# Softmax reciprocals that ride in the maximum's transposes and are spread over 128 partitions by a transfer inside SBUF

## The reference

```python
q = _lora_linear(hidden_states, Wq, Aq, Bq)      # 8 x 256 x 1024 -> 32 heads of 32
k = _lora_linear(traces, Wk, Ak, Bk)             # 8 heads, each serves 4 query heads
v = _lora_linear(traces, Wv, Av, Bv)
scores = jnp.einsum('bhqd,bhtd->bhqt', q, k) / jnp.sqrt(jnp.asarray(HD, q.dtype))
attn = jax.nn.softmax(scores, axis=-1)
context = jnp.einsum('bhqt,bhtd->bhqd', attn, v)
out = _lora_linear(context, Wo, Ao, Bo)
return hidden_states + out
```

## Time and profile before

| what | value |
|---|---|
| median of 3 runs | 734.06 us (733.98 to 735.76) |
| the profiled execution | 734.93 us |
| its span | 733.1 us |
| PE busy | 715.6 us (98%) |
| DVE busy | 465.7 us (64%) |
| ACT busy | 446.6 us (61%) |
| POOL busy | 246.4 us (34%) |

### The profile page before, as it was taken

One profiled execution on the slowest core, in us unless ns is written; L12 is line 12 of the kernel. 1 busy time (PEld: TensorE's weight loads), 2 busy tenths in 40 slices (PEclk: granted clock), 3 DMA queues, 4 the chain that ended last, 5 costly groups with the idle time before them and its releaser, 6 DMA issues.

```text
span 733.1 us, 15768 instructions
## 1 busy us (share of the span) xinstructions
PE 715.6 (98%) x5248; PEld 611.6 (83%) x5248; DVE 465.7 (64%) x833; ACT 446.6 (61%) x1418; POOL 246.4 (34%) x246
## 2 busy tenths in 40 slices
PE   6989999999999999999999999999989999999998
PEld 6768888888888888888888888888757788888886
DVE  4947877787777777678678778778876321222211
ACT  3547788788878878878788878788976211011100
POOL 3662731550641245165134406505456300000000
PEclk8999999999999999999999999999989999999999
DMA  6777663465356346435735733654674533454231
GB/s 234 268 226 191 186 178 120 123 195 174 109 179 199 124 152 188 142 98 176 202 109 157 200 122 115 196 175 137 188 228 138 187 129 113 161 172 138 91 114 57
DMA packets 94785, 117.10 MB, mean 160 GB/s; under 512 B 8736, under 2 KB 76320, under 8 KB 94752
## 3 DMA queue, kind: packets, MB, share of 16 engines
q1 hardware_dynamic: 94752, 116.69, 51.0%
HBM read 78.91 MB, written 37.75 MB: 159 GB/s over the span
## 4 chain that ended last, share of the span: by engine, by line
PE 89%; DVE 4%; ACT 3%; DMA 2%; issue 1%; POOL 1%; SPq 0%; DVEq 0%
PE banks L1043 34%; PE banks L1116 23%; PE banks L1061 9%; PE banks L1105 9%; PE banks L1086 8%; PE banks L1096 2%; PE banks L1077 2%; ACT banks L706 1%; PE banks L1028 1%; DMA probs_t<-b4kv 1%; DVE w_sum L827 1%; PE banks L1030 1%; DVE neg_max L857 1%; POOL k_stack L583 1%; DMA probs_t<-wq 1%
## 5 line engine op out<-in xcount | busy, mean ns | idle before, releaser
L706 ACT ACTIVATE banks<-banks,neg_max 128x256 f32<-128x256 f32 x512 | 229.2, 449 | 63.5 <-DVE neg_max L857 63.5
L857 DVE TENSOR_REDUCE neg_max<-banks 128x2 f32<-128x512 f32 x256 | 175.7, 687 | 53.0 <-PE banks L1061 51.0
L717 ACT ACTIVATE probs_t<-banks 128x512 f32<-128x512 f32 x256 | 154.3, 603 | 44.8 <-PE banks L1086 44.3
L1043 PE MATMUL banks<-x_hi,w_hi 128*128 128x256 f32 x512 | 144.8, 283 | 1.2 <-DVE q_stage L850 0.7
L1043 PE MATMUL banks<-x_lo,w_hi 128*128 128x256 f32 x512 | 144.8, 283 | 0.0
L1043 PE MATMUL banks<-x_hi,w_lo 128*128 128x256 f32 x512 | 144.6, 282 | 0.0
L633 POOL TENSOR_TENSOR rsum_cols<-rsums,ones 128x256 f32<-128x256 f32 x64 | 39.5, 618 | 220.4 <-PE banks L1096 220.2
L1061 PE MATMUL banks<-k_stack,q_stack 96*128 96x256 f32 x512 | 110.1, 296 | 1.6 <-ACT banks L706 1.2
L1086 PE MATMUL banks<-q_stack,k_stack 104*128 104x512 f32 x256 | 107.9, 421 | 0.0
L706 ACT ACTIVATION_READ_ACCUMULATOR banks<-banks,neg_max 128x1 f32 x512 | 104.8, 205 | 0.0
L1061 PEld LDWEIGHTS banks<-k_stack,q_stack 96*128 96x128 f32 x512 | 79.7, 190 | 29.1 <-ACT banks L706 14.7
(11 more groups left out here) (109 smaller groups left out, 1393.4 us busy)
## 6 DMA issues: line engine op xcount, KB each, us to landing
q_stack<-q_parts SPq DMA_DIRECT2D x192, 128.0 KB, 2.6
q_parts<-q_stage SPq DMA_DIRECT2D x64, 256.0 KB, 2.2
raw<-ct SPq DMA_DIRECT2D x32, 256.0 KB, 5.1
raw<-xt SPq DMA_DIRECT2D x32, 256.0 KB, 4.4
context<-ctx_stage SPq DMA_DIRECT2D x64, 128.0 KB, 2.1
stage<-xn SPq DMA_DIRECT2D x16, 512.0 KB, 4.2
w_hi<-context SPq DMA_DIRECT2D x14, 512.0 KB, 6.0
out<-raw SPq DMA_DIRECT2D x13, 512.0 KB, 2.9
```

Source lines behind the costliest of these rows:

```text
L706: last = nc.scalar.activation(score_bank[c % 2][:, S * h:S * (h + 1)], score_bank[c % 2][:, S * h:S * (h + 1)], ACT.Exp, bias=neg_max[:, u ...
L717: nc.scalar.activation(probs_t[:, u % 2, t, 2 * hp:2 * hp + 2, :].rearrange("p a b -> p (a b)"), st_bank[j % 2], ACT.Exp, scale=-1.0).then ...
L857: nc.vector.tensor_reduce(out=neg_max[:, u % 2, 2 * c:2 * c + 2], in_=score_bank[c % 2].rearrange("p (h t) -> p h t", h=2), axis=AXIS, op= ...
L1043: mm = nc.tensor.matmul(proj_bank[bank][:, 0:S], lhs, rhs, start=(k == 0), stop=(k == GROUP_MM - 1))
```

## The change

The reciprocals are written into columns 0 to 3 of the two halves of `max_parts`, so that the transposes of the next unit's maximum turn them too: rows 0 to 3 of the turned tile then hold the reciprocals of the 4 heads, 256 queries each. VectorE copies these four rows to `r_rows` in SBUF (`copy_rsums`, c = 3), and SP issues a transfer from SBUF to SBUF that writes each of the four rows to 32 partitions of `scales` (`spread`). `normalize` multiplies by `scales` as before, but without the copy, and stands in slot c = 3 in place of c = 1. `widen`, its tile and the two transposes in `context` are gone. `scales` and `r_rows` have two buffers. After the last unit there is one more turn, for the last reciprocals.

```diff
+        r_rows = sb("r_rows", [GH, 2, S], F32)
+        scales = sb("scales", [P, 2, S], F32)
...
+                def spread(g):
+
+                    if first and g < 0:
+                        return
+                    wait(r_copied, unit0 + (g + 1))
+                    need(sp, ctx_done, unit0 + (g - 1))
+                    sp.dma_start(scales[:, g % 2], r_rows[:, g % 2].unsqueeze(1).broadcast_to([GH, HD, S])
+                                 ).then_inc(r_spread[g % 2], DMA)
...
                 stack_q(3, fills + 2, st0)
                 stack_k(1, b + 1, st0)
-                store_ctx(-1)
+                spread(-1)
+                store_ctx(-2)
                 send(pos["q", 4, 0])
                 stack_q(4, fills + 3, st0 + 4)
+                spread(0)
+                store_ctx(-1)
                 send(pos["q", 5, 0])
-                store_ctx(0)
                 for j in range(4):
                     wait(c_ready, b * 4 + (j + 5))
                     load_inputs(xt, b + 1, j)
                 send(pos["q", 6, 0])
                 stack_q(5, fills + 3, st0 + 8)
+                spread(1)
+                store_ctx(0)
                 send(pos["q", 7, 0])
-                store_ctx(1)
                 stack_q(6, fills + 4, st0 + 12)
+                spread(2)
...
-            def widen(b, u):
-
-                pool.wait_ge(rsum_done, b * NG + (u + 1))
-                need(pool, rsum_turned, b * NG + u)
-                wide = rsums[:, u % 2, :].unsqueeze(2).broadcast_to([P, 2 * GH, HD])
-                nc.gpsimd.tensor_tensor(rsum_cols[:], wide, ones[:].unsqueeze(2).broadcast_to([P, 2 * GH, HD]), ALU.mult).then_inc(rsum_wide, 1)
...
             def reciprocal(b, u):
+
                 dve.wait_ge(exp_done, b * SLOTS + (4 * u + 4))
-                need(dve, rsum_wide, b * NG + (u - 1))
-                nc.vector.reciprocal(rsums[:, u % 2, :], sums[:, u % 2, :]).then_inc(rsum_done, 1)
+                dve.wait_ge(max_turned, b * NG + (u + 1))
+                nc.vector.reciprocal(max_parts[:, :, 0:GH],
+                                     sums[:, u % 2, :].rearrange("p (a h) -> p a h", a=2)).then_inc(rsum_done, 1)
+
+            def copy_rsums(b, u):
+
+                dve.wait_ge(max_turned, b * NG + (u + 2))
+                dve.wait_ge(r_spread[u % 2], b * (4 * DMA) + DMA * (u // 2 + 1))
+                nc.vector.tensor_copy(r_rows[:, u % 2, :], turned[0:GH]).then_inc(r_copied, 1)
 
             def normalize(b, u):
-                dve.wait_ge(rsum_turned, b * NG + (u + 1))
-                need(dve, ctx_done, b * NG + u)
-                nc.vector.tensor_copy(scales[:], scale_rows).then_inc(scales_done, 1)
-                dve.wait_ge(scales_done, b * NG + (u + 1))
+                dve.wait_ge(r_spread[u % 2], b * (4 * DMA) + DMA * (u // 2 + 2))
                 dve.wait_ge(ctx_mm, b * NG + (u + 1))
                 dve.wait_ge(ctx_stored[u % 2], b * (4 * DMA) + DMA * (u // 2 + 1))
-                nc.vector.tensor_tensor(ctx_stage[:, u % 2, :], ctx_bank, scales[:],
+                nc.vector.tensor_tensor(ctx_stage[:, u % 2, :], ctx_bank, scales[:, u % 2, :],
                                         ALU.mult).then_inc(ctx_done, 1)
...
-                if c == 1 and not (first and u < 2):
-                    normalize(b, u - 2)
                 if c == 2 and here:
                     place_max(b, u)
+                if c == 3 and not (first and u < 1) and not (last and u > NG):
+                    copy_rsums(b, u - 1)
                 if c == 3 and here:
                     reciprocal(b, u)
+                if c == 3 and not (first and u < 2):
+                    normalize(b, u - 2)
...
             def context(b, u):
 
-                pe.wait_ge(rsum_wide, b * NG + (u + 1))
                 need(pe, ctx_done, b * NG + u)
-                for qh in range(2):
-                    last = nc.tensor.transpose(
-                        scale_rows[:, P * qh:P * (qh + 1)],
-                        rsum_cols[:, GH * qh:GH * (qh + 1), :].rearrange("p h d -> p (h d)"), ident[:])
-                last.then_inc(rsum_turned, 1)
                 pe.wait_ge(st_exp, b * SLOTS + (4 * u + 4))
```

More of the change, by code:

```diff
@@ L140, in xattn @@
         ctx_bank = banks[:, 4, 0:S]
-        scale_rows = banks[:, 5, 0:S]
-        max_rows = banks[0:KM, 5, S:2 * S]
+        turned = banks[0:KM, 5, 0:S]
         proj_bank = [banks[:, 6 + i, :] for i in range(2)]
@@ L196, in xattn @@
         rsum_done = sem("rsum_done")
-        rsum_wide = sem("rsum_wide")
-        rsum_turned = sem("rsum_turned")
-        scales_done = sem("scales_done")
+        r_copied = sem("r_copied")
+        r_spread = [sem(f"r_spread{i}") for i in range(2)]
         v_moved = sem("v_moved")
@@ L399, in _ @@
                 sp.sem_inc(ctx_stored[i], DMA)
+                sp.sem_inc(r_spread[i], DMA)
             def body(b, first, last):
@@ L422, in body @@
                 if last:
-                    last_body(b, fills, st0, store_ctx, lambda g: send(pos["q", g, 0]))
+                    last_body(b, fills, st0, spread, store_ctx, lambda g: send(pos["q", g, 0]))
                     return
@@ L468, in load_context, with last_body @@
                                      ).then_inc(raw_in[j], DMA)
-            def last_body(b, fills, st0, store_ctx, send):
+            def last_body(b, fills, st0, spread, store_ctx, send):
                 def late_loads(*chunks):
@@ L502, in last_body @@
                 stack_q(7, fills + 4, st0 + 16)
+                spread(3)
                 late_loads(12)
@@ L506, in last_body @@
                     load_rows(0, h)
-                store_ctx(3)
+                store_ctx(2)
                 late_loads(13, 14)
@@ L512, in last_body @@
                     load_ctx(v, v % 2)
+                spread(4)
                 late_loads(15)
+                store_ctx(3)
+                spread(5)
                 store_ctx(4)
+                store_first(0)
+                spread(6)
                 store_ctx(5)
-                store_first(0)
+                store_first(1)
+                spread(7)
                 store_ctx(6)
-                store_first(1)
                 store_ctx(7)
@@ L626, in first_split @@
                                         ALU.subtract).then_inc(o_ready if j == 3 else first_lo, 1)
-            def widen(b, u):
-                pool.wait_ge(rsum_done, b * NG + (u + 1))
-                need(pool, rsum_turned, b * NG + u)
-                wide = rsums[:, u % 2, :].unsqueeze(2).broadcast_to([P, 2 * GH, HD])
-                nc.gpsimd.tensor_tensor(rsum_cols[:], wide, ones[:].unsqueeze(2).broadcast_to([P, 2 * GH, HD]), ALU.mult).then_inc(rsum_wide, 1)
             def slot(b, s, first, last):
                 u, c = divmod(s, 4)
-                if c == 1 and not (first and u < 1):
-                    widen(b, u - 1)
                 if s in (3, 4, 6, 7):
@@ L875, in place_max @@
                 nc.vector.tensor_tensor(q_stack[rows, u % RING],
-                                        max_rows[rows].unsqueeze(1).broadcast_to([M_ROWS, GH, S]),
+                                        turned[rows].unsqueeze(1).broadcast_to([M_ROWS, GH, S]),
                                         head_mask[rows].unsqueeze(2).broadcast_to([M_ROWS, GH, S]),
@@ L974, in _ @@
                     slot(b, s, False, False)
-            for s in range(FIRST, SLOTS + 6):
+            for s in range(FIRST, SLOTS + 8):
                 slot(NB - 1, s, False, True)
@@ L1070, in stacks_ready, with turn_max @@
                     pe.wait_ge(k_stacked[g // 4], b * (3 * DMA) + 3 * DMA)
-            def turn_max(b, u):
-                pe.wait_ge(max_split, b * NG + (u + 1))
+            def turn_max(b, u, drained):
+                if not drained:
+                    pe.wait_ge(max_split, b * NG + (u + 1))
+                need(pe, rsum_done, b * NG + u)
                 need(pe, max_placed, b * NG + u)
-                need(pe, scales_done, b * NG + (u - 1))
+                need(pe, r_copied, b * NG + (u - 1))
                 for qh in range(2):
-                    last = nc.tensor.transpose(max_rows[:, P * qh:P * (qh + 1)], max_parts[:, qh, :], ident[:])
+                    last = nc.tensor.transpose(turned[:, P * qh:P * (qh + 1)], max_parts[:, qh, :], ident[:])
                 last.then_inc(max_turned, 1)
@@ L1151, in slot @@
                 u, c = divmod(s, 4)
-                if c == 2 and u >= 0 and not (last and u >= NG):
-                    turn_max(b, u)
+                if c == 2 and u >= 0:
+                    turn_max(b, u, last and u >= NG)
                 if not (first and u < 1) and not (last and u > NG):
```

31 lines of the change are left out of this document (18 added, 13 removed).

## The result

The changed kernel takes 838.26 us (median of 4 runs, 834.39 to 839.84) against 734.02 us for the kernel before in the same session: a ratio of 1.1408, 95% interval 1.1364 to 1.1451. That is 104 us slower; the forecast was 777 us in a range from 716 to 806. The profiled execution has a span of 836.6 us.

What follows compares the result with a forecast made beforehand. PE's instructions were taken to bound the loop at 7.83 us a unit; 8.55 us was forecast, so 56 units x 0.72 = 40 us plus 2 for the last batch on 734.9 gave 777 us, range 716 to 806.

Steps and rivals of the forecast that it cites:

- the rival that was taken: Late spread in the attention loop: units of 8.0 to 9.1 us, 745 to 806 us in all; chance 0.53.
- the disputed cost: Engine time of each unit's spread, taken as 4.9 us between ends of 2.0 and 8.1, landing 6.5 us after issue.
- I take the middle, 8.55: Unit time in the attention loop, set midway between 8.2 and 8.9 us, 0.72 above the present 7.83.
- 8.2 us a unit by latency: Attention loop: a bare unit of 7.56 us plus 0.6, half the mean 1.2 us by which spreads land late.
- 8.9 by the engines: Attention loop: engines carrying the spread have 4.0 us of other work per unit and 4.9 more, 8.9 us.
- the delay that the spread gives to what stands behind it in SP's queue: SP's queue in the loop: delay to q_stack loads behind the spread, named as counted by neither limit; no size given.
- later landings of `q_stack`: Sign of a late spread in the loop: q_stack loads would land later; no size given.
- the last batch was given 2: Last batch: units of uneven length, some long enough to hide the spread, so only 2 us lost.
- The rule that half of a miss stays: Attention loop: a stall delays the next copy, giving the next transfer more time, so 1.2 us becomes 0.6 a unit.
- PE's saving: Two transposes per unit leave PE: 0.23 to 0.31 us, taken as 0.27, over 64 units 17.3 us.
- DVE's lateness: Multiply in slot c = 3 just ahead of the context product: up to 0.2 us every other unit, 3 us (0 to 6).
- POOL and the end of the kernel: POOL loses widen with no effect; at the end about 11 us of PE products cover the last spread.

Runs made afterwards that it cites:

- the chain: Kernel before plus, after its last store, seven groups of 8 SBUF-to-SBUF transfers of 128 KB from differing source partitions, each waited for; 940.24 us.
- spread_first: Changed kernel, rows still on partitions 0 to 3, with each spread ahead of stack_q and the loads in SP's queue; 797.09 us, ratio 1.0822.
- idle_neighbours: Kernel before plus a spread per unit from partitions 0 to 3, constant tile to spare tile, only the next spread waiting for it; 840.03 us, ratio 1.1431.
- no_spread: Changed kernel without the spread transfer; SP raises the semaphore instead and scales is filled once with 0.01; 723.76 us, ratio 0.9852.
- apart_first: Changed kernel with the four rows on partitions 0, 4, 8, 12 and each spread early in SP's queue; 724.24 us, ratio 0.9859.
- rows_32: Changed kernel with each reciprocal written to 8 columns, so the spread reads 32 partitions, each row 4 times; 735.93 us, ratio 1.0028.
- idle_half: Kernel before plus a spread per unit that no multiply waits for, sending only 128 of 256 columns; 741.38 us, ratio 1.0104.

## Why the prediction was wrong

**Right: the direction, the rival that was taken, and the size of the disputed cost.** The spread was assumed to take 4.9 us of engine time on four engines; the chain has 4.6. Landing 6.5 us after issue was assumed; the chain has 6.89 and the changed kernel 7.3 on average where the multiply waits for it. The size was partly luck: 4.9 came from the middle of 2.0 and 8.1 and from the landing of `k_stack`, which measures something else.

**Wrong: the step "I take the middle, 8.55".** Two limits had been worked out, 8.2 us a unit by latency and 8.9 by the engines, and averaged. They are not two estimates of one thing. The larger is a floor, and what has to be judged is how much comes on top. With the measured 4.6 the floor is 8.6; spread_first, with the spreads early in the queue, is at 8.78. The changed kernel has 9.46, 0.7 more, and that part goes away with the order of SP's queue. So of the 0.91 us between 8.55 and 9.46 the averaging explains at most 0.35 (8.9 in place of 8.55), and the next point the rest.

**Wrong with it: the delay that the spread gives to what stands behind it in SP's queue, put at nothing.** It had been named in the forecast ("neither counts the delay that the spread gives to `q_stack` loads behind it") and then given no number. In the unit shown, the store behind a spread takes SP 3.62 us to issue; the q_parts land in 5.1 us (median) instead of 2.2, `stack_q` waits for them, and the next spread stands behind `stack_q`. The delay from the end of the copy to the issue was put at 3.3 and 1.5 us from the earlier trace rows; over the loop it is 3.5 on average, from nothing to 6.3. The rows before could give it only for a queue that is not held up. The sign that was named for this, later landings of `q_stack`, did not come (2.7 us against 2.6): these loads are issued late, they do not land slowly.

In microseconds: the 56 units outside the last batch were given 0.72 each, 40 us. The 47 of the loop cost 1.61 each, and the first 55 units 87.9. The last nine units took 15.7 where the last batch was given 2; three of its short units carry 13.0 of that, of 6.8, 7.2 and 7.6 us, which became 10.2, 10.3 and 14.2. The forecast had counted on the long units there to hide the spread; these short ones lie under the floor.

**Wrong in form: by how latency works.** The rule that half of a miss stays gives, with the measured 4.0 us from the start of the copy to the issue and 7.3 to the landing, (11.3 - 7.9) / 2 = 1.7 and a unit of 9.3; it would have come out near the truth. That would have been luck: in idle_neighbours no multiply waits for the spread, and the loss is as large.

**Not foreseen: the clock.** PE is busy 383.65 us in 444 us of loop, 8.17 us a unit, where no_spread needs 7.60 at a granted clock of 1.00. So of the 9.46 us, 7.60 are PE's work, 0.57 is put down to its slower clock after waits (0.93 over the loop), and 1.29 are waiting. In a kernel that waits for its queue this is not all loss; part of it only takes the place of waiting. How much was not separated.

**PE's saving: 0.23 to 0.31 forecast, 0.27 taken.** Measured in no_spread 7.61 against 7.85, 0.24. The lower end was right: the context product follows the last projection product by 0.21 us in no_spread, just over the 0.12 to 0.20 that had been named, where one projection product follows another by 0.12. So part of the 0.31 us was a change-over that stays. Over the whole kernel no_spread gains 10 us and not 64 x 0.24 = 15; four units of the first batch take 8.4 to 9.0 us there (7.8 to 8.1 before), with short waits for ACT, and that was only seen, not tested.

**DVE's lateness: 3 us forecast, none in the loop.** The copy of 4 x 256 takes 0.40 us as assumed, yet the multiply is in time at 7.60 us a unit in no_spread and apart_first. The slack is thin, as the short waits of rows_32 suggest.

**POOL and the end of the kernel: as forecast.** POOL is busy 39 us less and nothing follows; after the last unit's context product both kernels need the same 157 us.

The better version of the change is apart_first: rows on partitions 0, 4, 8, 12 and the spread ahead of the loads, 724.24 us against 734.31, 1.4% faster than the kernel before.

## What to carry to other kernels

A transfer's cost is not only when it lands but what it holds meanwhile: ask for its engine time per period beside the other transfers' busy time, take that sum as a floor, and never average it with a limit that lies under it. Then ask what the transfer does to the issue of everything behind it in its queue. A mean DMA share of 0.5 does not say that there is room, if the new transfer loads a few engines or one part of the SBUF. To see whether a transfer hurts by being late or by being there, add it to the kernel before with nobody waiting for it; that run separated the two here.

## What the runs showed of the hardware

- A transfer inside SBUF that reads few partitions many times is limited by which partitions they are: waited for one by one (chains), 128 KB from rows 0 to 3 take 6.89 us, from rows 0, 4, 8, 12 3.10 us, from all 128 2.09 us.
- Behind the transfer from rows 0 to 3, SP's later issues can be held: four loads of 256 KB took 6.37 us to issue instead of 1.91 (idle_neighbours), and 17 of the changed kernel's 64 context stores took over 1 us, up to 3.74, where one did before. At half the bytes (idle_half) the loop's unit does not change.
- After a wait of 3.77 us the granted clock of the next 5 us was 0.50 (1.2 GHz), where the 5 us before the wait had 1.00; the same 16 products took 1.94 us instead of 1.07.
- DVE's reciprocal takes 191 ns for 8 columns and 541 ns for 64 (rows_32); a copy of 256 columns from PSUM takes 0.40 us on 4, 16 or 32 partitions alike.
